# A two-layer decoder on one core: four hand-written engine orders replaced by another set, same pieces

## The reference, cut to what matters

```python
x = x + mla(ln(x))              # L0 attn: 16 heads of 16, low-rank k and v, rotation by head index, softmax over 256 keys
x = x + head_attn(ln(x), ctx)   # L0 xattn: per token, 16 heads of 64 attend to each other's k and v
x = x + mod_ffn(ln(x))          # L0 ffn: the top 128 of 256 tokens by a router go through 256->1024->256 with gelu, times a gate
x = x + sparse_attn(ln(x))      # L1 attn: 16 heads of 16; all but the 25 largest scores of a row are set to 0 before softmax
x = x + masked_attn(ln(x), ctx) # L1 xattn: 16 heads of 16, keys masked by length
x = x + ternary(ln(x))          # L1 ffn: x @ sign-quantized weight * alpha + bias
```

## Time and profile before

| what | us |
|---|---|
| median of 3 runs (lowest to highest) | 6607.57 (6584.87 to 6625.48) |
| the profiled execution, its time | 6607.57 |
| its span | 6605.8 |
| PE busy in it | 5836.5 (88%) |
| DVE busy | 4544.8 (69%) |
| ACT busy | 4002.7 (61%) |
| POOL busy | 1507.1 (23%) |
| one full pass of the loop, 29 of them | 187.0 to 198.2 |

### The profile page before, as it was taken

How to read it: one execution, slowest core, us unless ns; L and a number is a source line. 1 busy time by engine, 2 the same in 40 slices (tenths; PEclk the granted TensorE clock), 3 DMA queues, 4 the chain that set the end, 5 groups by cost and what they waited for, 6 DMA issues and landing times. The chain is left out here.

```text
span 6605.8 us, 109636 instructions
## 1 busy us (share of the span) xinstructions
PE 5836.5 (88%) x37478; PEld 3841.2 (58%) x37762; DVE 4544.8 (69%) x16186; ACT 4002.7 (61%) x9761; POOL 1507.1 (23%) x2564
## 2 busy tenths in 40 slices
PE   6899899899898899898899898899999899989875
PEld 3566566566566556556556556556655656656542
DVE  1476776767777767677767677767677767677663
ACT  2565666655676665666665666656666666566632
POOL 0122222222222222222222222212222212222211
PEclk7898999988899998898998898989899989889875
DMA  2000000000000000000000000000000000000000
GB/s 80 4 6 5 8 6 8 8 6 5 8 6 8 8 6 5 8 6 8 8 6 5 8 6 8 8 6 5 8 6 8 8 6 8 5 8 6 4 4 4
DMA packets 29456, 54.18 MB, mean 8 GB/s; under 512 B 8145, under 2 KB 9810, under 8 KB 27986
## 3 DMA queue, kind: packets, MB, share of 16 engines
q1 hardware_dynamic: 28770, 45.73, 2.2%
HBM read 37.33 MB, written 8.39 MB: 7 GB/s over the span
## 5 line engine op out<-in xcount | busy, mean ns | idle before, releaser
L351 DVE TENSOR_REDUCE m_nm<-bankM 128x2 f32<-128x512 f32 x1024 | 672.8, 683 | 623.5 <-PE bankM L341 623.5
L915 POOL TENSOR_TENSOR t_pr<-t_pr,sc 128x512 f32<-128x512 f32 x512 | 650.3, 1270 | 1530.4 <-ACT t_pr L840 1529.5
L888 DVE MATCH_REPLACE8 wk<-m,wk 128x256 f32<-128x256 f32 x2048 | 819.6, 406 | 0.0
L884 DVE MAX8 m<-wk 128x8 f32<-128x256 f32 x2048 | 755.5, 409 | 0.0
L341 PE MATMUL bankM<-m_kT,m_q 32*128 32x256 f32 x4096 | 712.8, 474 | 28.9 <-DVE m_nm L351 22.0
L395 PE MATMUL bankM<-m_q,m_kT 32*128 32x512 f32 x2048 | 626.2, 690 | 0.0
L846 ACT ACTIVATE t_pr<-t_pr,t_nm 128x256 f32<-128x256 f32 x1024 | 463.6, 502 | 190.6 <-POOL t_pr L915 184.9
L341 PEld LDWEIGHTS bankM<-m_kT,m_q 32*128 32x128 f32 x4096 | 420.5, 220 | 250.1 <-issue 167.4
L909 POOL TENSOR_SCALAR mx<-m 128x2 f32<-128x2 f32 x512 | 115.4, 225 | 1875.5 <-DVE wk L888 1872.7
L652 ACT ACTIVATE xk_area<-bankH,xb 64x256 f32<-64x256 f32 x1024 | 480.5, 469 | 93.5 <-PE bankH L547 74.6
L884 DVE MAX8 m<-sc 128x8 f32<-128x256 f32 x1024 | 381.3, 413 | 162.0 <-ACT sc L831 142.1
(11 more groups left out here) (207 smaller groups left out, 11852.7 us busy)
## 6 DMA issues: line engine op xcount, KB each, us to landing
xin<-x_in SPq DMA_DIRECT2D x32, 256.0 KB, 3.8
ctxA<-ctx_in SPq DMA_DIRECT2D x32, 256.0 KB, 4.0
ctxB<-ctx_in SPq DMA_DIRECT2D x32, 256.0 KB, 3.5
out<-x SPq DMA_DIRECT2D x32, 256.0 KB, 2.0
w<-w_w SPq DMA_DIRECT2D x2, 1024.0 KB
xwq<-w_xwq SPq DMA_DIRECT2D x1, 1024.0 KB
xwk<-w_xwk SPq DMA_DIRECT2D x1, 1024.0 KB
xwv<-w_xwv SPq DMA_DIRECT2D x1, 1024.0 KB
```

Source lines behind the costliest of these rows:

```text
L351: nc.vector.tensor_reduce(b["nm"][:, i % 2, 2 * (i // 2) + x, :], banks[u % 3][:].rearrange("p (j s) -> p j s", j=2), AX.X, ALU.max, negat ...
L884: link.inc(nc.vector.max(top, src[:, t, :]))
L888: m = nc.vector.match_replace(out=wk[:, k, t, :], in_to_replace=take, in_values=src[:, t, :], imm_value=-BIG)
L915: nc.gpsimd.tensor_tensor(sp_[:, u % 2], taken[:, u % 2], sc[:, u % 3], ALU.mult).then_inc(g["sp_mul"], 1)
```

## The change

The four strings of `ORDER` are written anew. Each letter occurs as often as before on each engine, so each engine runs the same instructions; only their order differs. Nothing else changes. One line less in the table moves every later line number by one: L341 of before is L340 in the changed kernel, and so on. The first two lines of PE's string, and the first of the others:

```diff
     "pe": runs("""
-        m t c h3 c2 h t c t c t c t h c t h2 c h2 c h t c h c h2 c h2 t h t h c2 t h c2 h t c2 h c t c2 h t c2 t h2 c4 t c2 h c h c t h t h
-        t c h2 t c h c h2 t m t m t m h m t h m h m t h m t h m h t h m h2 m t h m h m t m t m t h m2 h m2 t m4 t h t h2 m2 h4 m t h m h3 t
+        t h c m h2 c t h2 t h t h t h2 c h2 t h2 c h2 t h c h2 t c t h c t h c h c t c h2 c t h c t2 h2 c h c3 t c2 h2 c2 h c2 t c h2 t c3 t
+        h c2 h2 c t h c3 h t h t h t h3 c t h m c t m2 t h m t h m2 t m2 h m t h m h m t h6 m t h2 m h t m4 t m2 t m3 t m5 t m t m t m t m t"""),
...
     "act": runs("""
-        h c2 t c2 t c t2 h t3 h t2 h2 t2 h2 t h6 t h t h2 t h t h t h2 t h3 t h t h3 c3 t2 h3 t c2 t3 h c2 h2 t c2 h3 t c2 h t h m h2 c3 h2
+        t h c m h4 c2 t h3 t7 h4 t h t h3 c h2 t h t h2 t h c h t3 h3 t h3 t h3 t h t h t2 h3 t h4 t3 h4 t h t h4 t h t2 h c3 h2 t c2 h3 t c2 t2
...
     "dve": runs("""
-        h t h c2 t h t c2 h c t c2 t c t c2 t3 c t m c t c3 t c2 t c2 t3 c t c t7 h t2 h4 t3 h t h t3 c3 t2 h2 t2 c3 h2 c t m t m t m h c t6
+        t h c m t h t h c t h c3 t12 c2 t2 c2 t h c2 t h c2 t h c2 h t c2 t c2 h2 t c2 t2 h2 t3 h t4 h2 t4 h2 t2 h2 t c3 t h t2 c t c t c t
...
     "pool": runs("""
-        t c h2 t c2 t h t8 c t3 h t4 h2 t3 h t3 m t c2 h c t3 m2 h t6 h3 t5 m t h2 t h t11"""),
+        t h c m t h t h t h c2 t10 h t2 h c t3 h t h t h t3 h t3 h t h t2 c2 t3 c t m2 t2 h3 t6 m t10"""),
```

More of the change, by code:

```diff
@@ L60 @@
     "pe": runs("""
-        m t c h3 c2 h t c t c t c t h c t h2 c h2 c h t c h c h2 c h2 t h t h c2 t h c2 h t c2 h c t c2 h t c2 t h2 c4 t c2 h c h c t h t h
-        t c h2 t c h c h2 t m t m t m h m t h m h m t h m t h m h t h m h2 m t h m h m t m t m t h m2 h m2 t m4 t h t h2 m2 h4 m t h m h3 t
-        m2 t m t h m t m t"""),
+        t h c m h2 c t h2 t h t h t h2 c h2 t h2 c h2 t h c h2 t c t h c t h c h c t c h2 c t h c t2 h2 c h c3 t c2 h2 c2 h c2 t c h2 t c3 t
+        h c2 h2 c t h c3 h t h t h t h3 c t h m c t m2 t h m t h m2 t m2 h m t h m h m t h6 m t h2 m h t m4 t m2 t m3 t m5 t m t m t m t m t"""),
     "act": runs("""
-        h c2 t c2 t c t2 h t3 h t2 h2 t2 h2 t h6 t h t h2 t h t h t h2 t h3 t h t h3 c3 t2 h3 t c2 t3 h c2 h2 t c2 h3 t c2 h t h m h2 c3 h2
-        t h t c2 h t h c2 t2 c t h3 t c t h t h3 t2 h2 t h t2 h c t h4 t h t m h3 m t m t2 m2 t h2 t3 h t h3 t h3 t h t h t h t h t h t3 m t
-        m2 t m2 t h t m2 t h m2 t3 h m2 t m t m h m t2 h2 t m2 t2 m t m h t m t m t"""),
+        t h c m h4 c2 t h3 t7 h4 t h t h3 c h2 t h t h2 t h c h t3 h3 t h3 t h t h t2 h3 t h4 t3 h4 t h t h4 t h t2 h c3 h2 t c2 h3 t c2 t2
+        h2 c2 h2 t c2 h2 t c3 h t h4 c2 t2 h c2 t h c t h2 t h t h c h t h t h t h t h t h t h c t4 m t m4 t h t2 h t h t4 h2 t h t m t2 h t
+        m2 t3 m2 t m2 t m2 t2 m2 t m3 t2 m2 t m2 t m t m t"""),
     "dve": runs("""
-        h t h c2 t h t c2 h c t c2 t c t c2 t3 c t m c t c3 t c2 t c2 t3 c t c t7 h t2 h4 t3 h t h t3 c3 t2 h2 t2 c3 h2 c t m t m t m h c t6
-        m t m2 h2 m3 t m h2 t m2 t m2 t m3 t2 m2 t2 h3 t2 h t4 h5 t2 h2 t3 h t3 m3 t3 m h2 t"""),
+        t h c m t h t h c t h c3 t12 c2 t2 c2 t h c2 t h c2 t h c2 h t c2 t c2 h2 t c2 t2 h2 t3 h t4 h2 t4 h2 t2 h2 t c3 t h t2 c t c t c t
+        c t m t m t m t2 h t c h t h2 m2 t m2 h2 m2 h2 m2 h3 m2 t m2 t2 m2 t m2 t3 h2 t2 h t6 m3 t3 m t"""),
     "pool": runs("""
-        t c h2 t c2 t h t8 c t3 h t4 h2 t3 h t3 m t c2 h c t3 m2 h t6 h3 t5 m t h2 t h t11"""),
+        t h c m t h t h t h c2 t10 h t2 h c t3 h t h t h t3 h t3 h t h t2 c2 t3 c t m2 t2 h3 t6 m t10"""),
 }
```

## The result

The changed kernel takes 6775.5 us (median of 4 runs, 6767.83 to 6799.49), the kernel before 6596.22 in the same comparison (4 runs, 6579.03 to 6625.48). The ratio is 1.0273, 95% interval 1.0224 to 1.0323: slower, by 179 us where the forecast had 115 (6723 us), and inside its range.

The account below looks back on a forecast made before the run. PE was taken as the bound, losing time to waits and half clock. Pairs 3.0, waits 3.7 and clock -3 gave +3.7 us a pass, x 29 = +107, plus 8 for short passes: 6607.6 + 115 = 6723 us, range 6470 to 6950.

Parts of the forecast that it names:

- the six short passes: Passes outside the 29 full ones: +17 us by share of time, halved to +8 for fewer streams and adjacencies.
- Part 1, the pairs: Matmuls on different array halves that ran side by side on PE: net three pairs lost at 1.06 us, +3.0 a pass.
- Part 2, waits: PE's waits inside a full pass, followed place by place: 17.0 us against 13.3 before, +3.7 a pass.
- c14: PE piece now directly behind c13: waits for c13's exponentials without t9 and h17 as cover, +1.4 us a pass.
- the chain h37, h40, h41: Pieces of h on PE forming a chain with ACT copies: 1.6 us of waits a pass.
- the bare steps m16, m22, m26 and m23: Steps of m left with one value block or one transpose as cover: 2.8 us of PE waits a pass.
- c9 to c13 with t13 and h26: Pieces c9, c10, t13, c12 and c13, with only small pieces as cover: 2.1 us of PE waits.
- m7 and h45: PE's waits behind m's adjacent score blocks m7/m8: 0.9 us put there.
- the first 50 us: Start of a pass, all 12 projections of h before h18: 2.0 us of PE waits at h16, t8 and h18 together.
- Part 3, the clock: Half-clock stretch from m's score blocks shrinks from 27 to about 15 us, less 2 for new falls: -3 us a pass.
- the second low stretch: Rival: clock falls at c12 to c14, stays low until h42, and again at m5; +16.7 us a pass, 7092; chance 0.12.
- The low clock: Rival: it goes, as full-size matmuls among m's score blocks keep the clock up; -3.3 us a pass, 6508; chance 0.23.

Follow-up runs that it names:

- run 1: Changed kernel with the new order only in the 29 full loop passes and the old order in the six short passes; ratio 1.0244 to the kernel before.
- run 2: Kernel before, with one PE piece moved one place at four spots so that no matmul pairs run side by side; ratio 1.0558.
- run 3: Changed kernel with t13 moved between c13 and c14 on PE, and t29 and t30 later on ACT; ratio 1.0225 to the kernel before.
- run 6: Kernel before, with c12 one place earlier on PE and its copy c5 two earlier on ACT, removing c13's wait; 6246.79 us, ratio 0.9472.
- run 5: Kernel before, with DVE's t46 moved behind m6 so the maxima of m's score block come earlier; ratio 0.9767.
- run 10: Kernel before, with t18 moved behind c32 on PE so that c32 waits longer; ratio 1.0032.
- run 9: Kernel before, with run 6's edit and also c32 moved behind h29 on PE to cover its wait; ratio 0.9542.
- run 4: Changed kernel with t18, h36 and t19 placed among c29 to c31 on PE as cover, and ACT's c24 behind h71; ratio 1.0546 to the kernel before.
- run 8: Changed kernel with DVE's t53 moved behind m7; ratio 1.0321 to the kernel before.
- run 12: Changed kernel with h44 moved between m5 and m6 on PE; ratio 1.0124 to the kernel before.

## Why the prediction was right, and where it was not

- **Direction and size.** Slower was forecast, and by +3.7 us a pass; the loop shows +3.88. That the two agree so well is in part luck: the waits were put 0.9 us too high and the clock's gain 1.3 us too high, and these misses cancel. The step from pass to kernel failed: the six short passes were given +8 us and took +36.7, all of it in the opening (run 1). "Fewer streams mean fewer adjacencies" isn't borne out: both opening passes got more waits and a lower granted clock. The loop and the opening make 149 us. The other 30 of the 179 are the spread of executions: the changed kernel was profiled in one of 6756.82, 18.7 under its median, the kernel before in one of 6607.57, 11.4 over the 6596.22 of the comparison.
- **Part 1, the pairs**, +3.0: confirmed in mechanism by runs 2 and 3; t9, t13 and t29 now run by themselves (1.13 us for t13). Busy time in the loop rose by 1.11 a pass. PE was busy at half clock for 3.3 us less, which is worth about 1.7 at half of it, so 2.8 are left for the three pairs.
- **Part 2, waits**, +3.7: measured +2.77. Idle inside a mean pass is 15.5 us and not 17.0 (21.3 less the 5.8 of the barrier), against 12.8 before (18.5 less 5.7). c14 (1.35 for 1.4), c30 (1.14 for 1.15), c31 (0.69 for 0.63) came out as computed from the rows. So did the chain h37, h40, h41 (0.25 + 0.64 + 0.69 for 1.6), the bare steps m16, m22, m26 and m23 (3 x 0.60 + 1.16 for 2.8) and c9 to c13 with t13 and h26 (1.9 for 2.1). m6 was 1.39 for 0.9, m8 0.78 for 1.0, but m7 and h45 nothing for 0.9 in most passes. m1's wait went as said; c32's is 0.8 where 0.4 was put. Too high were the first 50 us: h16 0, h18 0.21 and t8 0.47 for 2.0, a figure that rested on the count of ACT's list up to h18.
- **Part 3, the clock**, -3: measured about -1.7, by the estimate above. The low stretch of m's score blocks shrank as named, from 27 us to 10 to 17, 14.5 in the mean; it ends within h46 in 18 passes, in the score block behind it (m10) in 9 and before h46 in 2. But the prediction counted 27 us for every pass before, and the old order has them in 22 of 29, which is 20.7 in the mean: 6.2 less and not 12. A new fall begins at c14 in every pass, 3.4 us in most and 13.7 to 20.5 in 6 of 29 (the pass of 207.31 above). Low time fell by 3.8 us a pass in all. The price per us was read wrongly too: the pass of 187.00 us has not "almost none" of low clock but 13.6 us of it (PEclk 0.96), so 10.96 us go with 20.4 us of difference and not with 27. The two errors pull opposite ways.
- **The clock term** rightly stayed in the sum: run 6 took 5.3% off, three quarters of it or more with no other cause in the trace than the clock.
- **What the prediction had wrong about the kernel before.** It read the fall at 120 us as a consequence of what runs there and of the waits of 0.17 and 0.41 us in the earlier trace rows, and built rivals on it. Run 6 keeps that piece of the list and its wait of 0.41, and the fall is gone from 28 passes; runs 5 and 10 also remove it, with edits at 118 us and at 97 us into the pass, and both have the fall at 66 us in its place. Sum of waits and place of the fall are not tied as the text had them. The forecast survived because both orders fall somewhere in each pass, and the difference of two bad clocks is small. The old order wasn't at the good end of what its list allows: its own pass of 187.00 us said so, and 184.2 is reached by run 6.

Of the rivals, the second low stretch did come, but in 6 of 29 passes, which take 206 to 207 us and not the 213.6 that rival gives (196.9 + 16.7); it lasts 13.7 to 20.5 us and ends in c's transposed scores, not at h42. The low clock didn't go.

**What is open.** Why a pass takes one pattern or another isn't settled. In run 5 the 12 passes without a stretch have the clock fall at their barrier 0.1 to 0.4 us after they start, 15 of the 16 others have it at 1.8 to 3.2; in run 9 the 25 good passes have it at 0.6 to 1.2, the three bad ones at 2.4 and 2.5. That looks like a matter of some tenths of a us in when a pass begins, and would fit that small edits far away change it. But in the old order both patterns occur with the same beginning (0.6 to 0.9), so this is not enough. Nor is the edit by itself enough: the first pass of run 6 and four of run 9 have the stretch at 121 to 125 us with c13's wait gone, and seven passes of the old order lack it with the wait there. A run that shifts the pass's start and nothing else wasn't made.

## What to carry to other kernels

Where the granted clock falls and rises within a pass, an order has to be timed, not summed: edits of a few pieces moved the time by -5.3% to +5.6%, of which the change in idle time was never 2% (in run 2 the lost pairs are another 2.2%). Look first for two passes of one execution that differ at the same instructions; their difference is what the clock holds. And before a piece is called cover, see on its other engines' lists that its input is ready one place earlier: in six of the runs here (3, 4, 5, 8, 9 and 12) the wait came back at a neighbour.

## What the runs showed of the hardware that was not expected

- A small edit can change the clock far behind it: with a wait of 1.83 us at 57 us into the pass removed, a low stretch of 27.3 us at 120 us was gone from all but the first pass. By what path isn't shown.
- A longer wait needn't cost anything: c32 at 2.71 instead of 2.05 gave 1.0032 (1.0005 to 1.0060). And of run 5's two kinds of pass the one that is 10 us longer has less idle time (17.0 against 18.4).
- Passes settle into repeating patterns within one execution: 196.3 and 186.1 us in turn (run 5), 209.8 and 196.6 (run 2), 28 alike (runs 6 and 12).
- The matmuls of a pair (32 rows each, different halves of the array, different banks of PSUM) run fully side by side (2443.23 and 2443.25 to 2444.31 in the earlier trace rows), and being parted cost the 1.06 us; in run 2 it also came with 6.3 us more low time a pass.
